# Transposing two heads of q at a time, with the duplicate written by VectorE's copies

## The reference

```python
def attention(q, k, v):           # 32 q heads, 8 key heads (KV), D = 32, G = 4 q heads per key head
    qh = q.reshape(B, S, KV, G, D).transpose(0, 2, 3, 1, 4)
    kh = k.reshape(B, S, KV, D).transpose(0, 2, 1, 3)
    vh = v.reshape(B, S, KV, D).transpose(0, 2, 1, 3)
    scores = jnp.einsum('bkgsd,bktd->bkgst', qh, kh) / sqrt(D)
    weights = softmax(scores, axis=-1)
    out = jnp.einsum('bkgst,bktd->bkgsd', weights, vh)
    return out.transpose(0, 3, 1, 2, 4).reshape(B, S, E)

x = x + attention(layernorm(x), ctx, ctx)
x = x + moe(layernorm(x))         # 8 experts, top 2 of them for each token
```

## Time and profile before

| | |
|---|---|
| median of 3 executions | 10740.04 us (10738.85 to 10741.26) |
| span of the profiled execution | 10739.9 us |
| TensorE busy | 9553.0 us, 89% |
| VectorE busy | 4781.9 us, 45% |
| ScalarE busy | 3291.4 us, 31% |
| GpSimd busy | 2489.5 us, 23% |
| from 410 to 4560 us: TensorE, VectorE, ScalarE, GpSimd busy | 3236.37, 3122.07, 2552.51, 1657.09 of 4150 us |
| mean granted clock of TensorE there | 0.89 of full speed |
| from 4560 us to the end: TensorE, VectorE busy | 6128.95, 1319.51 of 6179.9 us |

### The profile page before, as it was taken

How to read it: one execution, slowest core, us unless ns; L and a number is a source line. 1 busy time by engine, 2 the same in 40 slices (tenths; PEclk the granted TensorE clock), 3 DMA queues, 4 the chain that set the end, 5 groups by cost and what they waited for, 6 DMA issues and landing times. The chain is left out here.

```text
span 10739.9 us, 176790 instructions
## 1 busy us (share of the span) xinstructions
PE 9553.0 (89%) x57064; PEld 4727.4 (44%) x57064; DVE 4781.9 (45%) x10025; ACT 3291.4 (31%) x4986; POOL 2489.5 (23%) x4115
## 2 busy tenths in 40 slices
PE   4577878787778887699999999999999999999989
PEld 3333333333333333344444444444444444444457
DVE  7777777777777777622222222222222222222212
ACT  4466666666666666500000000000000000000001
POOL 0134443444344433411111111111111111111111
PEclk7799998899989989899999999999999999999999
DMA  9512221221222221154444444444444444444445
GB/s 366 198 70 74 72 72 68 72 75 69 72 72 73 72 72 70 57 193 169 169 170 170 170 170 166 165 170 165 170 170 170 169 166 168 170 168 170 170 149 174
DMA packets 479024, 1480.37 MB, mean 138 GB/s; under 512 B 100632, under 2 KB 121112, under 8 KB 478496
## 3 DMA queue, kind: packets, MB, share of 16 engines
q1 hardware_dynamic: 352928, 1073.63, 28.3%
q0 software_dynamic: 125696, 403.01, 9.9%
HBM read 1149.98 MB, written 349.49 MB: 140 GB/s over the span
## 5 line engine op out<-in xcount | busy, mean ns | idle before, releaser
L1409 PE MATMUL f_y<-f_xt,f_w 128*128 128x512 f16 x16896 | 3657.2, 379 | 0.8 <-DVE f_xt L1466 0.8
L1409 PEld LDWEIGHTS f_y<-f_xt,f_w 128*128 128x128 f16 x16896 | 1653.1, 98 | 1994.2 <-DVE f_xt L1466 1.0
L1426 PE MATMUL f_y<-f_w,f_yt 128*128 128x512 f16 x8704 | 1965.2, 379 | 0.4 <-DVE f_yt L1478 0.4
L1448 ACT ACTIVATE f_silu<-f_y,f_scales 128x512 f32<-128x512 f32 x320 | 219.8, 687 | 4598.3 <-PE f_y L1409 4471.6
L732 ACT ACTIVATE a_p<-a_sc,a_escale 128x512 f32<-128x512 f32 x2048 | 1370.8, 690 | 781.9 <-PE a_pv L565 406.1
L978 DVE TENSOR_REDUCE a_nmax<-a_mx 128x2 f32<-128x512 f32 x2048 | 1309.6, 682 | 332.1 <-PE a_mx L597 180.6
L597 PE MATMUL a_mx<-a_ks,a_qs 96*128 96x256 f16 x4096 | 774.5, 292 | 679.6 <-DVE a_nmax L978 671.7
L1426 PEld LDWEIGHTS f_y<-f_w,f_yt 128*128 128x128 f16 x8704 | 820.7, 98 | 922.4 <-DVE f_yt L1478 42.5
L565 PE MATMUL a_pv<-a_p,a_v 128*64 128x512 f32 x4096 | 1200.5, 666 | 9.8 <-ACT a_o L740 2.2
L1375 POOL DMA_INDIRECT out<-f_rows,f_idx_y x256 | 253.6, 991 | 4100.0 <-DVE f_rows L1509 4100.0
L1491 DVE SCALAR_TENSOR_TENSOR f_prod<-f_y,f_scales,f_silu 128x512 f32<-128x512 f32 x320 | 240.3, 751 | 2106.9 <-PE f_y L1409 1900.3
(11 more groups left out here) (197 smaller groups left out, 9442.3 us busy)
## 6 DMA issues: line engine op xcount, KB each, us to landing
f_w<-w_parts SPq DMA_DIRECT2D x1088, 512.0 KB, 3.4
w_parts<-w_parts SPq DMA_DIRECT2D x136, 512.0 KB, 4.8
h_w<-w_parts SPq DMA_DIRECT2D x136, 512.0 KB, 5.5
a_x<-in_x SPq DMA_DIRECT2D x64, 1024.0 KB, 5.1
a_xres<-in_x SPq DMA_DIRECT2D x64, 1024.0 KB, 5.1
out<-a_xres SPq DMA_DIRECT2D x64, 1024.0 KB, 4.0
xn_parts<-a_xhl SPq DMA_DIRECT2D x64, 1024.0 KB
w_in<-in_w SPq DMA_DIRECT2D x80, 512.0 KB, 8.6
```

What stands on the lines that cost most here:

```text
L1409: last = pe.matmul(y1[:, bank, :], w1b[:, j, t, pw, :], xT[:, px, t, :], start=n == 0, stop=n == 3 * HT - 1)
L1426: last = pe.matmul(y2[:, g % 2, :], yT[:, py, m, cols], w2b[:, m, pw, outs], start=m == 0 and py + pw == 0, stop=m == FULL and pw == 1)
```

## The change

`a_qsrc` gets a row of 64 per head in place of 128: high and low only. Two heads then lie in 128 neighbouring elements, and one transpose turns both. Four heads in two halves take four transposes into the first four of the eight blocks of `a_tr`: partitions 0 to 63 hold high and low of the first head, 64 to 127 those of the second. VectorE's copy sorts this into `a_qs`: for each of the two heads of a pair high and low go to partitions 0 to 63, and high once more to partitions 64 to 95. These are four copies of 512 elements per partition, two over 64 and two over 32 partitions. VectorE's copy of the high part within `a_qsrc` (L1054), its semaphore and TensorE's wait on it go, and so does GpSimd's memset of the zeros (L821).

```diff
-        qsrc = sb("a_qsrc", [P, 2, 2, NH, P], F16)
+        qsrc = sb("a_qsrc", [P, 2, 2, NH, 2 * D], F16)
...
-            pe.wait_ge(filled, 4)
+            pe.wait_ge(filled, 3)
...
                 at_least(pe, n["q_low"], b * 2 + 2)
-                at_least(pe, n["q_high2"], b * 2 + 2)
                 at_least(pe, n["q_there"], b * 8 + kv)
...
-                for g in range(G):
+                for gp in range(2):
                     for c in range(2):
-                        last = pe.transpose(TR[:, 2 * g + c, :], qsrc[:, 1 - par, c, kv * G + g, :], ident16[:, :])
+                        head = kv * G + 2 * gp
+                        last = pe.transpose(TR[:, 2 * gp + c, :],
+                                            qsrc[:, 1 - par, c, head:head + 2, :].rearrange("p a b -> p (a b)"),
+                                            ident16[:, :])
                 last.then_inc(n["q_turned"], 1)
...
-            act.wait_ge(filled, 4)
+            act.wait_ge(filled, 3)
...
-            pool.memset(qsrc[:, :, :, :, 3 * D:P], 0.0).then_inc(filled, 1)
...
-                    dve.tensor_copy(QS[0:96, 1 - par, kv, :], TR[0:96, :, :].rearrange("p a b -> p (a b)"))\
-                        .then_inc(n["q_there"], 1)
+                    for ab in range(2):
+                        for first, size, to in ((0, 2 * D, 0), (0, D, 2 * D)):
+                            src = TR[2 * D * ab + first:2 * D * ab + first + size, 0:4, :]\
+                                .rearrange("p (g c) s -> p g (c s)", c=2)
+                            dst = QS[to:to + size, 1 - par, kv, :].rearrange(
+                                "p (g ab cs) -> p g ab cs", g=2, ab=2)[:, :, ab, :]
+                            last = dve.tensor_copy(dst, src)
+                    last.then_inc(n["q_there"], 1)
...
-                if k in (4, 5) and on(i):
-                    c = k - 4
-                    dve.wait_ge(n["q_high"], i * 2 + (c + 1))
-                    dve.tensor_copy(qsrc[:, par, c, :, 2 * D:3 * D], qsrc[:, par, c, :, 0:D])\
-                        .then_inc(n["q_high2"], 1)
```

More of the change, by code:

```diff
@@ L427, in attend @@
         n = {}
-        for name in ("stats1", "aggr1", "rstd1", "nbias1", "xn_done", "q_high", "q_low", "q_high2",
+        for name in ("stats1", "aggr1", "rstd1", "nbias1", "xn_done", "q_high", "q_low",
                      "ctx_max", "ctx_all", "ctx_chain", "k_high", "k_low", "escaled", "v_made",
```

## The result

| | before | after |
|---|---|---|
| median | 10739.44 us (4 runs) | 10997.63 us (4 runs, 10993.27 to 11011.35) |
| ratio | | 1.0242, 95% interval 1.0228 to 1.0257 |
| span of the profiled execution | 10739.9 us | 10995.1 us |
| end of `attend` on: TensorE, VectorE busy | 6128.95, 1319.51 of 6179.9 us | 6128.02, 1319.48 of 6178.0 us |

A forecast was written before the change was run, and what follows sets the result against it. VectorE was taken to bound most attention steps, GpSimd's chain or queue others; TensorE fills the untouched rest. Batch terms 3.81 and 3.43 plus 1.16 gave 8.40 us a pass, 269 over 32 pairs: 10740 + 269 = 11009 us, range 10860 to 11110.

The forecast's parts named there:

- The copies' price: Four VectorE copies for one, no overlap: 1.16 us more per key head; rival with overlap 0.72, 10874 us, chance 0.22.
- The map of what bounds each step: Which engine ends last in each of a batch's eight key-head steps, k0 to k7; a loop pass holds two batches.
- k1 and k2: Key-head steps 1 and 2: 2.32 us of added copies hide under VectorE's 4.22 and 2.80 us idle.
- copy of k3: Key-head step 3, VectorE working without a gap: full 1.16 us in each batch.
- k4 to k6: Key-head steps 4 to 6: copies less the removed copy (0.34 us in each of two steps) and idle taken up.
- copy of k7: Key-head step 7, where TensorE waits for VectorE: full 1.16 us in each batch.
- k7 of the first batch to k2 of the second: Stretch within a pass bound by GpSimd's queue, 3.8 us to spare for VectorE: added copies cost nothing.
- k0 behind the jump: First batch's key-head step 0, after the loop's 4.56 us standstill, ahead of GpSimd's all-reduce: 1.16 us a pass.
- The idle time at the start of k5: VectorE's wait for TensorE as key-head step 5 begins, 0.76 and 1.20 us, which takes up added copy time.
- The clock: Rival: TensorE's k7 wait grows to 3.0 us, its clock falls, third maximum 1.1 us late: 11080 us, chance 0.22.
- one element a step: Rival: each new copy takes 0.68 us, 2.24 more per key head than now: 11384 us, chance 0.05.
- TensorE as the bound: Rival: fewer transposes save 0.23 us in the two steps where VectorE waits for TensorE: 10711 us, chance 0.04.

The follow-up runs named there:

- its part alone: Kernel before with four transposes of q per key head in place of eight, one copy kept: 10718.48 us, ratio 0.9988.
- the last four runs: Kernel before with q's copy on ScalarE in steps 3, 6, 7: 10715.72; also 0: 10700.56; GpSimd's subtractions earlier: 10682.36; that plus ScalarE in all four: 10662.85 us.

## Why the prediction was right, and where it was not

**The copies' price** held: 0.415 us long and 0.43 apart where 0.41 and 0.44 were taken, 1.14 more per key head for 1.16. Taking the dearer end because no row overlapped instructions on different partitions decided the forecast: with 0.33 it would have been 10874, and the run with all copies from partition 0 shows that this is where such copies come out (+176 for 169).

**The map of what bounds each step** held in the main: nothing in k1 and k2, about one copy a pass in k0, the jump unchanged, and from k3 to k7 VectorE's work. By the table of distances, the sum's terms came out so, in us a pass:

| stretch | forecast, first and second batch | measured |
|---|---|---|
| copy of k3 (k2-3) | 1.16, 1.16 | 0.67, 1.03 |
| k4 to k6 (k3-4, k4-5, k5-6) | 1.49, 1.11 | 1.12, 1.18 |
| copy of k7 (k6-7) | 1.16, 1.16 | 1.54, 1.48 |
| k7 of the first batch to k2 of the second | 0 | 0.00 |
| k0 behind the jump (k7-0, k0-1, k1-2) | 1.16 | 1.13 + 0.73 - 0.84 = 1.02 |
| sum | 8.40 | 8.04 |

The all-reduce of the second batch still ends 9 us behind GpSimd's last slot DMA, as the rows that answer show (2708.38 against 2699.46):

```profile
2698.51 0.95 POOL L892 DMA_INDIRECT slots<-a_entry,a_slot_ix  x1 [0.30 <-issue]
...
2708.00 0.38 POOL L850 PARTITION_ALL_REDUCE a_call<-a_cmax  x1 [8.53 <-issue]
```

**k3** was the weak term, too large by 0.62 us a pass, 20 us. The prediction has VectorE working without a gap there. In the kernel before this is not so: TensorE comes out of its wait at the low clock, and VectorE waits for it a little and stretches its maxima (1.46 us for the pair in place of 1.29):

```profile
2525.25 0.61 PE L597 MATMUL a_mx<-a_ks,a_qs 96*128 96x256 f16 x2 [6.64 <-DVE a_nmax L978]
```

```profile
2525.98 1.46 DVE L978 TENSOR_REDUCE a_nmax<-a_mx 128x2 f32<-128x512 f32 x2 [0.19 <-PE a_mx L597]
```

In the first batch the changed kernel shortens TensorE's wait in k3 from 5.61 to 3.50 us in the mean, and the pair of matmuls behind it from 0.61 to 0.44: the clock gives time back here. The run with the copies in steps 1 and 2 alone shows the same without any edit in k3: the wait is 3.26 us, the pair 0.47, and k2-3 of the first batch 0.32 us shorter. In the second batch the wait did not shrink (4.54 before, 4.97 after), and the price was nearly full.

**The idle time at the start of k5** was read from a single pass: 0.76 us in the first batch, which is the low end there of 27 passes (0.76 to 1.34, mean 1.08). With the mean the sum for k4 to k6 of that batch is 1.17 where 1.12 was measured. That is 0.37 us a pass, 12 us. In the second batch the pass read had 1.20 (mean 1.01), and since TensorE's own delay was taken as the bound there, the sum held.

**The clock** was priced as a rival and came in part. TensorE's wait in k7 is 2.85 us (3.0 forecast). The rows of k7, first and second batch, answer:

```profile
2684.85 0.39 PE L597 MATMUL a_mx<-a_ks,a_qs 96*128 96x256 f16 x2 [2.85 <-DVE a_nmax L979]
...
2750.83 0.61 PE L597 MATMUL a_mx<-a_ks,a_qs 96*128 96x256 f16 x2 [2.85 <-DVE a_nmax L979]
```

At 0.61 the granted clock is the lower level, 1.2 against 2.4 GHz. Of 59 rows in the stage with such a wait of 2.6 to 2.95 us, nearly all k7's, 42 have a pair above 0.5 us. So the premise was right in most batches, but not the price of 1.1 us. It was built on a third pair that comes 5.41 us after the first. In the 54 k7's of the table it came that late in 14, and there the third maximum waited, 0.80 us at 2756.91; in the other 40 it came after 4.3 to 4.7 us, and the maximum waited less than 0.3 us. In the 14 the small instruction behind (2758.51) took 0.19 in place of 0.81, since VectorE now came behind GpSimd's subtraction, which gave most of the wait back. So k7-0 grew by 1.18 and 1.13, no more than the copy of k0. What the clock did cost is in k6-7, 1.54 and 1.48 for 1.16: the router's part up to the third maximum of k6 is unchanged (5.06 us), the copies are 1.15 longer, and the four maxima around TensorE's wait take 2.80 and 2.75 us where they took 2.40. That is 0.35 us a batch more than the sum had, 22 us in all.

**What cancelled.** In the sum k3 was 20 us too large, k4 to k6 of the first batch 12 and k0 4, k4 to k6 of the second 2 too small; the clock in k7 (22 us) was left out. The net is 11 us, which is why 11009 met 10998 to 0.1%. That is luck in part: the single terms were off by up to 0.5 us of 1.16.

**The other rivals**: one element a step (11384) is out by the length of 0.415. TensorE as the bound (10711) is out; its part alone gave 11 us.

**What the forecast overlooked** did no harm to it: GpSimd's standstills in steps 6 and 7 are in the time of both kernels. They mislead about a change that moves work away from VectorE there, as they did, in part, in the last four runs.

## What to carry to other kernels

Price an edit on a busy engine from start to start, not by length, and ask of each new instruction whether it starts at the same partitions as its neighbour: the 0.10 us of lost overlap here come on top of 0.33, a third of a short copy's price. Then mark in which stretches of the pipeline the engine is the one waited for; four short copies cost nothing in two steps and nearly their whole price in three others. Read idle times from many passes, not from one. Before moving work off an engine, look for single instructions far longer than their kind: where one waits for another engine, what is taken off ahead of it is not gained.

## What the runs showed of the hardware that I had not expected

- A VectorE instruction over 16 elements per partition, 0.17 us elsewhere, took 1.85 to 2.07 us in the rows shown, beside a GpSimd subtraction. In the kernel before, all 110 of these instructions and those over 32 that took over 0.6 us ended within 0.06 us of the end of a subtraction.
- Behind the loop's jump VectorE stands 3.7 to 4.6 us in the kernel before, 4.25 in the mean. In the kernel with the four copies in step 0 alone a second standstill came two instructions later, 2.52 us in the row shown and 2.3 us a pass on average; its cause is open.
- With the output's start partition changing between copies, and the input's not, VectorE's copies start 0.43 us apart in place of 0.33; 32, 64 or 96 partitions make next to no difference in length (0.41 to 0.42).
- More VectorE work in two steps made the next one 0.32 us shorter: TensorE's wait ahead of it went from 5.61 to 3.26 us, and its matmuls behind the wait ran faster (0.47 us for a pair in place of 0.61).
